# Gather the base from the output itself, ask for the expert weights before the third store, places ahead of gates, scatters in two halves

## The chip, the cores and the metric

One core of one Trainium2 chip runs the whole kernel. The metric is the device time of an execution in microseconds (us). TensorE does the matmuls and transposes, VectorE (DVE), ScalarE (ACT) and GpSimd (POOL) the rest; SyncE (SP) issues most DMAs, GpSimd the indirect ones. Each engine runs its own instruction list in order, and the lists are tied together by semaphores written out by hand.

## The reference, cut to what matters

x is (16, 128, 256): 16 blocks b of 128 channels and 256 positions. Read as rows it is 2048 tokens of 256 values.

```python
# part 1: long convolution of outer products, gated into x
kv  = einsum('bhil,bhjl->bijhl', k, v)            # k = v = ctx, heads of 8
y   = irfft(rfft(kv, 512) * rfft(kernel, 512))[..., :L] + kv * D
x   = x + tanh(g_xattn) * einsum('bijhl,bhil->bjhl', y, layernorm(x))
# part 2: mixture of 8 experts, one per token, capacity 256, and a shared expert
xt = layernorm(x).reshape(2048, 256)
probs = softmax(xt @ Wg); eidx = argmax(probs); gate = probs[eidx]
pos  = (cumsum(onehot) * onehot).sum(-1) - 1; keep = pos < 256
xd   = rows of xt placed at slot eidx * 256 + pos (kept tokens)
oe   = (silu(xd @ W1[e]) * (xd @ W3[e])) @ W2[e]
shared = (silu(xt @ sw1) * (xt @ sw3)) @ sw2
x = x + tanh(g_ffn) * (oe of the token's slot * gate * keep + shared)
```

## The kernel before

The 16 blocks are taken in 4 groups (NG) of 4. The program is a list of slots: slots s = 0 to 31 (CONV) each hold one unit of the convolution (convolve on TensorE, products on VectorE, the kv products of the next group on GpSimd and ScalarE); slots 32 to 50 hold the rest of the shared expert. Inside the slots every step of a group has a due slot (STEPS, for the last group LAST_STEPS): turn the summed terms back and add them to x (turn_r, residual), second layer norm into xrow (ln2), transpose (turn_xT, tokens_low), logits and choice of the expert (choose), gate (gate), place in the expert (places, slot_of_token), scatter.

The steps of the change:

- **Terms and folds.** For groups 2 and 3 the eight terms are folded to four by GpSimd (fold, line 606), one fold a slot; TensorE's turn_r for these groups waits for 8 and for 16 folds.
- **Choice.** gate writes the gate value beside each token's row in xrow (column 256), slot_of_token computes the row numbers dest; its second operation (line 899) frees the PSUM bank of the places, which a later transpose needs. Column 257 of xrow is the token's number (iota). For each of the 4 blocks GpSimd then issues one indirect DMA that scatters 128 rows of 258 floats to xd_scratch (line 639), after it has waited for dest_done and gate_done. For groups 0 to 3 this is due in slots 20, 28, 36 and 42.
- **Shared expert.** Token blocks n = 0 to 7 of 256 tokens: up projection chunks ("gu", n, c), then ("y", n, 0), which VectorE adds to x_sb (line 920). SyncE then stores the two blocks of x_sb twice: to out and to base_scratch (line 549).
- **Experts.** Blocks 8 to 15 are experts 0 to 7. Each weight set is loaded by four DMAs (line 495 twice, 506, 508) into one of 5 buffers that lie in the memory of the terms, so the first load waits for the last turn_r. In SyncE's list the first five experts' loads stand after the stores of n = 2. The weights are split into a high part (ScalarE, weights_high, line 765) and a low part (VectorE, weights_low, line 956) for w = e + 1; w = 1 has its own slot, w = 2 and later follow the first chunk of the expert before. Each matmul of line 1148 runs three times (high x high, low x high, high x low).
- **Rows.** SyncE loads an expert's 256 rows from xd_scratch (load_rows, line 420), the first two after the stores of n = 5 and once all scatters have landed. TensorE transposes them (turn_xe, line 1183; for experts 0 and 1 in slots 49 and 50, from XE_SLOT on), ScalarE and VectorE split them (xe_high, expert_tokens_low), VectorE takes the token numbers from them (tokens_of_slots, tok).
- **Ends.** gather(e) fetches the tokens' rows from base_scratch (line 654), gather(0) waits for all 16 stores; VectorE adds gate times expert output (line 932), and an indirect DMA scatters the sum to out (line 665).

Of the kernel before, what the change touches and what calls it, by code (L numbers as in the profile page):

```python
# [195 lines left out]

def build(nc, x, ctxt, kpad, skip_d, g_x, g_f, wg, w1, w3, w2, sw1, sw3, sw2, out):
    xd = nc.dram_tensor("xd_scratch", (E * CAP, ROW), F32, kind="Internal").ap()
    base = nc.dram_tensor("base_scratch", (B * CH, L), F32, kind="Internal").ap()
    kskip = nc.dram_tensor("kskip_scratch", (H, KPAD), F32, kind="Internal").ap()  # L200
    out_rows = out.rearrange("b c l -> (b c) l")

    with ExitStack() as ctx:
# [265 lines left out]
        def _(sp):  # L469
# [74 lines left out]
                sp.dma_start(xd_flat[k], zeros).then_inc(xd_zeroed, 16)  # L544
            load_ctx(3)
            for n in range(8):
                sp.wait_ge(f_free, FU_AT[("y", n, 0)] + 1)
                for dst in (out, base.rearrange("(b c) l -> b c l", c=CH)):
                    sp.dma_start(dst[2 * n:2 * n + 2].rearrange("b c l -> c b l"),
                                 x_sb[:, 2 * n:2 * n + 2, :]).then_inc(base_stored, 16)  # L550
                if n == 2:
                    for e in range(SETS):
                        load_expert(e)
                if n == 5:
                    for e in range(2):
                        load_rows(sp, e)
# [8 lines left out]
        def _(pool):  # L565
# [35 lines left out]
            def fold(s):  # L601
# [3 lines left out]
                             for i in range(2))  # L605
                pool.tensor_tensor(low, low, high, ALU.add).then_inc(folded, 1)  # L606

            def split_up():
                pool.wait_ge(w_high, 1)
                up = slice(2 * HP, 4 * HP)  # L610
                pool.tensor_tensor(wl_gu[0][:, up], shared_gu[:, up], plain(wh_gu[0][:, up]),
                                   ALU.subtract).then_inc(w_low_pool, 1)

            for s in range(SLOTS):
# [9 lines left out]
                if s == SLOTS - 1:  # L624
                    pool.wait_ge(z_ready, CONV)
                    pool.memset(bg[:, :, :, :], 0.0).then_inc(pool_consts, 1)
                g = due("scatter", s)
                if g >= 0:
                    if g == 0:
                        pool.wait_ge(xd_zeroed, 16 * 4)  # L630
                    if g >= 2:
                        pool.wait_ge(scattered[g % 2], 16 * GB)
                    pool.iota(xrow[:, g % 2, :, L + 1:L + 2], pattern=[[P, GB], [1, 1]], base=1 + g * GB * P,
                              channel_multiplier=1, allow_small_or_imprecise_dtypes=True).then_inc(numbered, 1)
                    pool.wait_ge(numbered, g + 1)
                    pool.wait_ge(dest_done, g + 1)
                    pool.wait_ge(gate_done, g + 1)
                    for b in range(GB * g, GB * (g + 1)):
                        pool.indirect_dma_start(  # L639
                            out=xd, out_offset=bass.IndirectOffsetOnAxis(ap=dest[:, b:b + 1], axis=0),  # L640
                            in_=xrow[:, g % 2, b % GB, :], in_offset=None, bounds_check=E * CAP - 1,
                            oob_is_err=False).then_inc(scattered[g % 2], 16)
                if s == SPLIT_SLOT:
                    split_up()

            def gather(e):
                pool.wait_ge(tok_done, e + 1)
                if e == 0:
                    pool.wait_ge(base_stored, 16 * 16)
                    pool.wait_ge(pool_consts, 6)  # L650
                if e >= BRING:
                    pool.wait_ge(f_free, FU_AT[("y", 8 + e - BRING, 0)] + 1)
                for t in range(2):
                    pool.indirect_dma_start(  # L654
                        out=bg[:, e % BRING, t, :], out_offset=None, in_=base,
                        in_offset=bass.IndirectOffsetOnAxis(ap=tok[:, e, t:t + 1], axis=0),
                        bounds_check=B * CH - 1, oob_is_err=False).then_inc(gathered[e % BRING], 16)

# [12 lines left out]
        def _(act):  # L671
# [104 lines left out]
            for s in range(SLOTS):  # L776
# [20 lines left out]
                    weights_high(1)  # L797
                if s >= XE_SLOT:
                    xe_high(s - XE_SLOT)
            for n in range(SHARED_USES, len(FU)):  # L800
                kind, blk, c = FU[n]
                silu(n)
                if kind == "gu" and c == 0 and blk + 1 < 16:
                    weights_high(blk + 1 - 7)
                if kind == "gu" and c == 1 and 10 <= blk + 1 < 16:
                    xe_high(blk + 1 - 8)

        @block.vector
        def _(dve):
# [186 lines left out]
            for s in range(SLOTS):  # L996
# [18 lines left out]
                    norm_stats(NORM_AT[("ln2", due("ln2_stats", s))])  # L1015
                if due("logits", s) >= 0:
                    choose(due("logits", s))
                if due("gate", s) >= 0:
                    gate(due("gate", s))
                if due("places", s) >= 0:  # L1020
                    slot_of_token(due("places", s))
                if s == SPLIT_SLOT:
                    weights_low(0)
                if s == EXPERT_SPLIT_SLOT:
# [1 line left out]
                if s >= XE_SLOT:  # L1026
                    expert_tokens_low(s - XE_SLOT)
                    tokens_of_slots(s - XE_SLOT)
            for n in range(SHARED_USES, len(FU)):
                kind, blk, c = FU[n]  # L1030
                feed_forward(n)
                if kind == "gu" and c == 0 and blk + 1 < 16:
                    weights_low(blk + 1 - 7)
                if kind == "gu" and c == 1 and 10 <= blk + 1 < 16:
                    expert_tokens_low(blk + 1 - 8)
# [205 lines left out]
```

## Time and profile before

| | |
|---|---|
| median of 3 runs | 228.96 us (228.89 to 229.14) |
| the profiled execution's own time | 228.0 us |
| its span, first to last instruction | 226.2 us |
| mean granted TensorE clock | 0.995 |
| busy: TensorE matmul / VectorE / ScalarE / GpSimd | 88% / 66% / 36% / 56% of the span |
| read / written in HBM | 21.32 / 10.54 MB |

The busy shares are of the whole span. Where the time is set is read from the chain of work that ended last and from what each engine waited for, stage by stage.

### The profile page before, as it was taken

To read this page: it belongs to the slowest core of one execution; us is meant where nothing else is said; L and a number is where in the kernel's file an instruction comes from. 1 tells how busy PE (TensorE), PEld (TensorE's weight loads), DVE (VectorE), ACT (ScalarE), POOL (GpSimd) and SP (SyncE) were. 2 spreads that over 40 slices of the span, in tenths; PEclk is the share of its full clock that TensorE was granted. 3 is DMA by queue.
4 is the path that set the end of the run, shared out by engine and by line. 5 is a ranking of instruction groups with operands and counts; after the bars stand their busy time and mean duration, and the time that the engine had idled before them with its cause. 6 is when DMAs were issued, how large, how long until landed. Compare 5 with 4: busy or idle time off the path is not lost.

```text
span 226.2 us, 3954 instructions
## 1 busy us (share of the span) xinstructions
PE 198.4 (88%) x1344; PEld 178.9 (79%) x1344; DVE 150.3 (66%) x483; ACT 80.7 (36%) x153; POOL 126.6 (56%) x129
## 2 busy tenths in 40 slices
PE   0399999969999898999989969997989999999970
PEld 0267789748998797898989959995989999999960
DVE  5868986699789885589855663752547755676240
ACT  2425314163460844033320653620352444234200
POOL 3797863395847489413690216083055677776651
PEclk9999999999999999999999999999999999999997
DMA  4799993000000010021300199995454888522221
GB/s 123 257 234 351 360 412 142 0 0 4 3 3 0 23 71 3 0 94 51 114 23 3 49 326 362 347 359 169 137 163 131 260 280 257 180 71 82 66 79 46
DMA packets 24101, 31.87 MB, mean 141 GB/s; under 512 B 3390, under 2 KB 21574, under 8 KB 24080
## 3 DMA queue, kind: packets, MB, share of 16 engines
q1 hardware_dynamic: 21424, 24.75, 33.7%
q0 software_dynamic: 2304, 6.05, 8.1%
q10 hardware_dynamic: 352, 0.81, 1.1%
q8 instruction: 11, 0.18, 0.3%
q14 instruction: 10, 0.08, 0.1%
HBM read 21.32 MB, written 10.54 MB: 141 GB/s over the span
## 4 chain that ended last, share of the span: by engine, by line
PE 66%; DVE 12%; DMA 8%; issue 5%; ACT 3%; POOL 2%; POOLq 1%; ACTq 0%; DVEq 0%; SPq 0%
PE fb L1148 13%; PE z L1148 10%; PE tp L1087 10%; PE z L1062 10%; PE z L1172 8%; PE z L1059 6%; DVE terms L452 5%; PE fb L1172 5%; DMA kskip_scratch<-kp 3%; DMA toep<-kskip_scratch 2%; DVE wl_gu L956 2%; DVE stats L824 2%; PE tp L1183 2%; POOL xd_scratch L639 1%; DMA xd_scratch<-xrow,dest 1%
## 5 line engine op out<-in xcount | busy, mean ns | idle before, releaser
L452 DVE TENSOR_TENSOR terms<-z,qr 128x512 f32<-128x512 f32 (+2 forms) x192 | 49.1, 326 | 8.0 <-PE z L1062 7.9
L1062 PE MATMUL z<-kv,toep 128*128 128x288 f32 x128 | 42.5, 415 | 0.0
L433 POOL TENSOR_TENSOR kv<-ct 128x768 f32<-128x768 f32 x15 | 28.2, 1883 | 13.9 <-PE z L1062 10.8
L1148 PE MATMUL fb<-xTh,wh_gu 128*128 128x256 f32 (+1 forms) x104 | 32.4, 312 | 0.7 <-issue 0.7
L1059 PEld LDWEIGHTS z<-kv,toep 128*128 128x128 f32 x128 | 22.7, 196 | 11.5 <-issue 7.7
L654 POOL DMA_INDIRECT kv<-base_scratch,tok x16 | 22.4, 1397 | 15.8 <-DMA base_scratch<-x_sb 11.3
L639 POOL DMA_INDIRECT xd_scratch<-xrow,dest x16 | 17.0, 1064 | 25.0 <-DVE dest L905 21.3
L1059 PE MATMUL z<-kv,toep 128*128 128x144 f32 x128 | 28.0, 302 | 2.9 <-DVE terms L452 2.4
L1148 PE MATMUL fb<-xTl,wh_gu 128*128 128x256 f32 (+1 forms) x104 | 29.1, 279 | 0.0
L1148 PE MATMUL fb<-xTh,wl_gu 128*128 128x256 f32 (+1 forms) x104 | 29.0, 279 | 0.0
L606 POOL TENSOR_TENSOR terms<-terms 128x512 f32<-128x512 f32 x16 | 20.2, 1282 | 11.3 <-DVE terms L452 11.3
L1148 PE MATMUL z<-xTh,wh_gu 128*128 128x256 f32 (+1 forms) x88 | 25.6, 291 | 0.8 <-DVE wl_gu L956 0.8
L1087 PE MATMUL tp<-ident,terms 128*128 128x128 f32 x192 | 23.0, 277 | 1.9 <-DVE terms L452 1.0
L1148 PE MATMUL z<-xTl,wh_gu 128*128 128x256 f32 (+1 forms) x88 | 24.5, 278 | 0.0
L1148 PE MATMUL z<-xTh,wl_gu 128*128 128x256 f32 (+1 forms) x88 | 24.4, 278 | 0.0
L1087 PEld LDWEIGHTS tp<-ident,terms 128*128 128x128 f32 x192 | 22.2, 193 | 2.5 <-DVE terms L452 1.2
L665 POOL DMA_INDIRECT out<-kv,tok x16 | 16.1, 1004 | 12.8 <-DVE kv L932 8.3
L744 ACT ACTIVATE sg<-fb 128x256 f32<-128x256 f32 (+1 forms) x26 | 9.8, 376 | 31.6 <-PE fb L1148 31.6
L1062 PEld LDWEIGHTS z<-kv,toep 128*128 128x128 f32 x128 | 20.6, 195 | 0.0
L1148 PEld LDWEIGHTS fb<-xTh,wh_gu 128*128 128x128 f32 (+1 forms) x104 | 19.3, 186 | 1.6 <-issue 0.9
L1148 PEld LDWEIGHTS fb<-xTh,wl_gu 128*128 128x128 f32 (+1 forms) x104 | 19.3, 185 | 0.8
L1148 PEld LDWEIGHTS fb<-xTl,wh_gu 128*128 128x128 f32 (+1 forms) x104 | 19.3, 186 | 0.0
(121 smaller groups left out, 377.9 us busy)
## 6 DMA issues: line engine op xcount, KB each, us to landing
terms<-w SPq DMA_DIRECT2D x16, 352.0 KB, 4.7
ct<-ctxt SPq DMA_DIRECT2D x3, 768.0 KB, 7.3
xd_scratch<-xrow SPq DMA_DIRECT2D x4, 516.0 KB, 9.4
kv<-xd_scratch SPq DMA_DIRECT2D x8, 258.0 KB, 3.5
out<-x_sb SPq DMA_DIRECT2D x8, 256.0 KB, 2.3
base_scratch<-x_sb SPq DMA_DIRECT2D x8, 256.0 KB, 2.9
terms<-w SPq DMA_DIRECT2D x8, 256.0 KB, 4.9
x_sb<-x SPq DMA_DIRECT2D x3, 512.0 KB, 6.1
```

The costliest lines, as they stand in the source:

```text
L433: eng.tensor_tensor(dst, left, right, ALU.mult)
L452: return eng.tensor_tensor(view(terms, t0 + row * TROW + col, [[64, 2], *td]), view(src, zo, [[512, 2], *zd]), view(qr, q0 + qo, [[CW, 2], ...
L606: pool.tensor_tensor(low, low, high, ALU.add).then_inc(folded, 1)
L639: pool.indirect_dma_start(out=xd, out_offset=bass.IndirectOffsetOnAxis(ap=dest[:, b:b + 1], axis=0), in_=xrow[:, g % 2, b % GB, :], in_off ...
L654: pool.indirect_dma_start(out=bg[:, e % BRING, t, :], out_offset=None, in_=base, in_offset=bass.IndirectOffsetOnAxis(ap=tok[:, e, t:t + 1] ...
L665: pool.indirect_dma_start(out=out_rows, out_offset=bass.IndirectOffsetOnAxis(ap=tok[:, e, t:t + 1], axis=0), in_=fin[:, e % 2, t, :], in_o ...
L744: act.activation(sg[0:n, k % SGS, :], bank[0:n, 0:256], ACT.Silu).then_inc(silu_done, 1)
L1059: pe.matmul(view(z[s % 2], k * 512 + GB, [[PL, NPL], [1, GB]]), toep[:, h, P:2 * P], view(kv, o, [[PL, NPL], [1, GB]]), start=True, stop=F ...
L1062: mm = pe.matmul(z[s % 2][:, k, 0:KVH], toep[:, h, 0:P], view(kv, o, [[1, KVH]]), start=False, stop=True, skip_group_check=True)
L1087: mm = pe.matmul(tp[n % 2][:, j * P:(j + 1) * P], src, ident[:, :], is_transpose=True, start=(t == 0), stop=(t == terms_of(g) - 1))
L1148: mm = pe.matmul(bank[0:rows(blk, c), m * 256:(m + 1) * 256], wt[w % 2][:, col:col + rows(blk, c)], xt[:, place, k, first:first + 256], st ...
L1172: mm = pe.matmul(bank[:, t * L:(t + 1) * L], hidden(blk, c)[0:rows(blk, c), t * P:(t + 1) * P], down[0:rows(blk, c), c * L:(c + 1) * L], s ...
```

## The change

Four edits.

1. base_scratch and its eight stores are gone; the gathers read the rows from out, and gather(0) waits for eight stores.
2. In SyncE's list the loads of the first five experts stand before the wait for ("y", 2, 0) and its store, not after it.
3. VectorE computes the places of a group before its gates. The split of expert 1's weights (w = 2) goes into the slots: its high part on ScalarE after xe_high(0), in slot XE_SLOT = 49, its low part on VectorE at the end of the last slot, 50, after tokens_of_slots(1).
4. The scatters of groups 0 to 2 go out in two halves: blocks 0 and 1 in the due slot, blocks 2 and 3 in the next one, behind that slot's kv products and fold. The last group's four stay together.

```diff
-    base = nc.dram_tensor("base_scratch", (B * CH, L), F32, kind="Internal").ap()
...
             for n in range(8):
-                sp.wait_ge(f_free, FU_AT[("y", n, 0)] + 1)
-                for dst in (out, base.rearrange("(b c) l -> b c l", c=CH)):
-                    sp.dma_start(dst[2 * n:2 * n + 2].rearrange("b c l -> c b l"),
-                                 x_sb[:, 2 * n:2 * n + 2, :]).then_inc(base_stored, 16)
                 if n == 2:
                     for e in range(SETS):
                         load_expert(e)
+                sp.wait_ge(f_free, FU_AT[("y", n, 0)] + 1)
+                sp.dma_start(out[2 * n:2 * n + 2].rearrange("b c l -> c b l"),
+                             x_sb[:, 2 * n:2 * n + 2, :]).then_inc(base_stored, 16)
...
+            def scatter(g, parts):
+                for b in parts:
+                    n = GB * g + b
+                    pool.indirect_dma_start(
+                        out=xd, out_offset=bass.IndirectOffsetOnAxis(ap=dest[:, n:n + 1], axis=0),
+                        in_=xrow[:, g % 2, b, :], in_offset=None, bounds_check=E * CAP - 1,
+                        oob_is_err=False).then_inc(scattered[g % 2], 16)
...
                 g = due("scatter", s)
+                if 0 <= due("scatter", s - 1) < NG - 1:
+                    scatter(due("scatter", s - 1), range(2, GB))
...
-                    for b in range(GB * g, GB * (g + 1)):
-                        pool.indirect_dma_start(
-                            out=xd, out_offset=bass.IndirectOffsetOnAxis(ap=dest[:, b:b + 1], axis=0),
-                            in_=xrow[:, g % 2, b % GB, :], in_offset=None, bounds_check=E * CAP - 1,
-                            oob_is_err=False).then_inc(scattered[g % 2], 16)
+                    scatter(g, range(GB if g == NG - 1 else 2))
...
-                    pool.wait_ge(base_stored, 16 * 16)
+                    pool.wait_ge(base_stored, 16 * 8)
...
-                        out=bg[:, e % BRING, t, :], out_offset=None, in_=base,
+                        out=bg[:, e % BRING, t, :], out_offset=None, in_=out_rows,
...
                 if s >= XE_SLOT:
                     xe_high(s - XE_SLOT)
+                if s == XE_SLOT:
+                    weights_high(2)
...
-                if kind == "gu" and c == 0 and blk + 1 < 16:
+                if kind == "gu" and c == 0 and 10 <= blk + 1 < 16:
                     weights_high(blk + 1 - 7)
...
+                if due("places", s) >= 0:
+                    slot_of_token(due("places", s))
                 if due("gate", s) >= 0:
                     gate(due("gate", s))
-                if due("places", s) >= 0:
-                    slot_of_token(due("places", s))
...
                     tokens_of_slots(s - XE_SLOT)
+                if s == SLOTS - 1:
+                    weights_low(2)
...
-                if kind == "gu" and c == 0 and blk + 1 < 16:
+                if kind == "gu" and c == 0 and 10 <= blk + 1 < 16:
                     weights_low(blk + 1 - 7)
```

## Rows read from the trace of the kernel before

**Rows 1.** The page's chain of work that ended last, by engine.

```profile
PE 66%; DVE 12%; DMA 8%; issue 5%; ACT 3%; POOL 2%; POOLq 1%; ACTq 0%; DVEq 0%; SPq 0%
```

**Rows 2.** The chain in order of time, from 112 us: start, us, what.

```profile
117.48 0.87 issue
...
152.03 3.07 DMA xd_scratch<-xrow,dest
...
155.16 2.66 DMA kv<-xd_scratch
```

**Rows 3.** TensorE's timeline where it waited: start, us, what [idle before <- releaser].

```profile
75.29 0.66 PE L1074 MATMUL tp<-ident,xn 128*128 128x128 f32 x4 [0.76 <-DVE t L899]
...
89.42 2.02 PE L1087 MATMUL tp<-ident,terms 128*128 128x128 f32 x16 [1.01 <-DVE terms L452]
...
133.30 0.66 PE L1097 MATMUL tp<-ident,xrow 128*128 128x128 f32 x4 [1.71 <-DVE t L899]
...
157.95 0.63 PE L1183 MATMUL tp<-ident,kv 128*128 128x128 f32 x4 [1.67 <-DMA kv<-xd_scratch]
...
166.49 0.36 PE L1148 MATMUL z<-xTh,wh_gu 128*128 128x256 f32 x1 [0.78 <-DVE wl_gu L956]
```

**Rows 4.** GpSimd's timeline, 85 to 119 us.

```profile
85.58 6.19 POOL L606 TENSOR_TENSOR terms<-terms 128x512 f32<-128x512 f32 x5
...
108.29 1.07 POOL L639 DMA_INDIRECT xd_scratch<-xrow,dest  x1 [3.21 <-DVE dest L905]
...
112.23 0.97 POOL L639 DMA_INDIRECT xd_scratch<-xrow,dest  x1 [0.30 <-issue]
113.22 5.03 POOL L606 TENSOR_TENSOR terms<-terms 128x512 f32<-128x512 f32 x4
```

**Rows 5.** Timelines of VectorE and GpSimd, 131 to 154 us.

```profile
131.93 0.42 DVE L915 TENSOR_TENSOR hT<-z,sg 128x256 f32<-128x256 f32 x1 [3.66 <-ACT sg L744]
...
134.69 1.28 DVE L943 TENSOR_TENSOR xTl<-tp,xTh 128x512 fp32r<-128x512 f32 x2
...
146.14 0.17 DVE L905 CAST dest<-slotf 128x4 int32<-128x4 f32 x1
...
147.99 1.61 DVE L956 TENSOR_TENSOR wl_gu<-terms,wh_gu 128x1408 fp32r<-128x1408 f32 x1
...
147.14 0.99 POOL L639 DMA_INDIRECT xd_scratch<-xrow,dest  x1 [7.11 <-DVE dest L905]
148.44 2.01 POOL L639 DMA_INDIRECT xd_scratch<-xrow,dest  x1 [0.30 <-issue]
```

**Rows 6.** Busy time by stretch; the last two columns are DMA share and GB/s.

```profile
118.00:122.00 4.00, 3.65 (x33) 3.69 (x34) 1.18 (x2) 0.15 (x1) 0.24 (x1) 1.00 0.01 4
...
150.00:154.00 4.00, 4.00 (x36) 3.95 (x35) 1.24 (x3) 1.04 (x3) 3.39 (x4) 1.00 0.91 318
```

**Rows 7.** Timelines of ScalarE and VectorE, 158 to 167 us.

```profile
158.62 0.60 ACT L750 ACTIVATE xTh<-tp 128x512 fp32r<-128x512 f32 x1 [4.50 <-PE tp L1183]
...
163.32 1.37 ACT L765 ACTIVATE wh_gu<-terms 128x1408 fp32r<-128x1408 f32 x1
...
163.08 0.16 DVE L964 SCALAR_TENSOR_TENSOR tok<-tv,kv 128x2 int32<-128x2 f32 x1
...
164.72 1.63 DVE L956 TENSOR_TENSOR wl_gu<-terms,wh_gu 128x1408 fp32r<-128x1408 f32 x1 [0.79 <-ACT wh_gu L765]
```

**Rows 8.** The page's DMA issues: operation, count, KB each, median us to landing.

```profile
out<-x_sb SPq DMA_DIRECT2D x8, 256.0 KB, 2.3
base_scratch<-x_sb SPq DMA_DIRECT2D x8, 256.0 KB, 2.9
```

**Rows 9.** SyncE's timeline, the first and the last of the 20 weight issues.

```profile
129.24 1.03 SPq L495 DMA_DIRECT2D terms<-w  x2
...
140.39 1.25 SPq L508 DMA_DIRECT2D terms<-w  x1
```

**Rows 10.** Line 639's landing times: the four scatters of group 1, then of group 3.

```profile
DMA to landing us min/median/max: 2.6/2.7/2.9
...
DMA to landing us min/median/max: 3.1/4.3/4.9
```

## The prediction

> **What bounds the kernel now.** I read the page's chain first [rows 1]: TensorE holds 66% of it, so most of the span is matmul time that this change doesn't touch. I then listed the chain in order of time from 112 us and looked only for pieces that aren't TensorE [rows 2]. Three places matter to this diff.
>
> First, TensorE waits twice for GpSimd. Before the residual transposes of group 2 it is idle 1.01 us [rows 3], and before those of group 3 the chain has 0.87 us at 117.48 [rows 2]. Both times GpSimd works without a pause from its first scatter (77.07 and 108.29) to the fold that is awaited: the third of the five from 85.58, at 85.58 + 3 x 6.19/5 = 89.3, and the last of the four from 113.22, at 118.25 [rows 4].
>
> Second, the stretch from the last group's places to the first expert. Group 3's dest is ready at 146.3, the four scatters run from 147.14 to 153.0, the last lands 3.07 us after its start, then SyncE asks for expert 0's rows (2.66 us to landing), and TensorE transposes them at 157.95 after 1.67 us of nothing [rows 2, 3, 5]. In that stretch the reader should see two handicaps: the second scatter takes 2.01 us where the others take 0.97, and it stands inside VectorE's 1.61 us weight split of line 956 [rows 5]; and the DMA engines are still 0.91 busy from 150 to 154, though idle from 118 to 122 [rows 6].
>
> Third, at 166.49 TensorE has waited 0.78 us for the low part of expert 1's weights (line 956) [rows 3]. After that the chain is TensorE without a gap, to expert 7's last matmul at 219.1.
>
> **The change, part by part.** The sum goes against the profiled execution: 228.0 us, span 226.2. The median of the three runs shown is 228.96, so I carry the difference 0.96 over to the forecast.
>
> *Expert 1's split earlier.* ScalarE made the high part at 163.32, behind the first expert silu, and VectorE the low part at 164.72, to about 166.35 [rows 7]. Now the high part stands behind xe_high(0), which ends at 159.2; its inputs are there (expert 1's loads are issued by 134, and the shared up-projection of block 7, the last reader of that half, ran before 153.7). It takes 1.37 us, to 160.6, and fits ahead of xe_high(1) at 161.65. The low part stands behind tok of expert 1, that is from 163.24, takes 1.63 and ends at 164.87. TensorE finishes the last chunk of expert 0 at 166.49 - 0.78 = 165.71, so its wait is gone: **-0.78**. Queued behind the low part is hT of (8,0), 163.51 before and 164.85 now; its readers are y of expert 0 (TensorE, 169.9) and the silu ring, both after 167. Covered by more than 2 us.
>
> A rule of the Trainium skill ("SBUF — State Buffer", section "SBUF: two separate sides") speaks against this move: VectorE with two SBUF inputs and GpSimd share a port pair that is locked for a whole instruction, whoever starts first, and the other blocks fully. The second scatter agrees, 2.01 against 0.97 us. By the rule a gather that started ahead of the split could push it back by up to 1 us and take back some 0.3 of the 0.78; but the gather can't start before y(7)'s store, issued at 162.07, has landed (2.3 us in the median [rows 8]), about 164.4, so the split is first.
>
> *No base copy.* Eight stores of 256 KB and their issues (0.47 to 0.53 us each on SyncE) go. The gathers wait for 8 stores, not 16; gather(0) started at 166.10, behind the last base store, and starts some 1.3 us earlier. Nothing waits: its reader at 172.7 has the data at about 171.6. Worth 0 by itself. The rows read are those of out before any expert scatter of the same token, so no new wait appears.
>
> *Weights ahead of the third store.* load_expert(0) waits for the last residual transposes, done at 122.2; before, it stood behind y(2)'s store at 128.30 and was issued at 129.24. Twenty issues take from 129.24 to 141.64, 12.4 us [rows 9], so now 122.2 to 134.6. Behind them in SyncE's queue stands y(2)'s store (ready at 128.3, issued about 134.6) and y(3)'s (134.8); only the gathers, 30 us later, wait for these. The first reader of the weights, at 145.97, never waited, so the earlier loads are worth nothing directly. Their worth is that with seven us of head start and 1.5 MB of base copies less the DMA engines are free when group 3 is scattered: 5.3 MB of weights and three 0.26 MB stores at about 350 KB/us end near 140. Scatters on idle engines land in 2.6 to 2.9 us (group 1), in the busy stretch in 3.1 to 4.9 [rows 10]. Only the last one is on the chain: 3.07 becomes about 2.7, **-0.4** (bounds 0 and -0.5). The load of expert 0's rows had 2.66, already the least of its kind, 0. The 1.04 us of the second scatter stay: the split of line 956 comes after the silu at 147.2 and meets it again.
>
> For that last scatter the Trainium skill ("DMA: Bandwidth & Descriptors", section "Anatomy of one DMA — SWDGE (gpsimd) path") gives 2.0 us plus bytes over 436 KB per us: for 132 KB 2.3 us, which would make this term -0.8. The rows of idle engines show 2.6 at the least, so the row is used.
>
> *Places ahead of gates.* Three gate operations and six places operations stand one behind the other on VectorE and end at 146.3 [rows 5]; the gates are 0.56 us of them. GpSimd waits for both results, and their sum is the same in either order: 0 for the scatters. What comes earlier by 0.56 us is the release of the transpose bank (line 899), for which TensorE waited 0.76 at 75.29 and 1.71 at 133.30 [rows 3]. Neither pays. At 75 what comes next is GpSimd's stretch from 77.07, which sets TensorE's start at 89.42 and begins when dest and gate are both done. At 133, TensorE's next need is the low part of the tokens, which VectorE ends at 135.97 after working from 131.93 without a pause [rows 5]; a permutation inside that stretch doesn't move its end. TensorE waits there longer instead. **0**; bounds -0.6 and 0.
>
> *Scatters in halves.* For groups 0 to 2 two scatters go out, then the next slot's products and fold, then two more. For group 2 nothing stands between. For 0 and 1 the same work has to be done before the awaited fold (scatters four, folds up to number 23 and up to 31), only in another order, so the end moves only by what a switch costs. Inside a run of scatters each one follows 0.30 us after the other's end; from scatter to fold there is no gap (112.23 + 0.97 = 113.20, fold at 113.22) [rows 4]. The trace has no scatter right behind a fold. Bounds: the 0.30 vanishes under the fold (-0.3 a group), or a restart costs what one costs after a wait, 0.83 from dest at 146.31 to 147.14 [rows 5], that is +0.5 a group. I take **0**, the 0.30 staying where it is: it stands ahead of a scatter after another scatter, and the nearest case is the same instruction.
>
> Sum: -0.78 - 0.4 = -1.2; 228.0 becomes 226.8, and with the 0.96 the median becomes **227.8 us**, -0.5%. Within 0.2% (0.46 us) a measurement of this kernel hardly tells from no change.
>
> **Rivals.**
> (a) *The halves pay.* If the switch hides the 0.30 twice, and the earlier bank release brings anything, both waits for GpSimd shrink: 227.8 - 0.6 = 227.2, at most 226.6. For it: both stretches really end in a wait of TensorE (1.01 and 0.87). Against: nothing shows the gap hidden.
> (b) *Only one term comes.* The last scatter still lands in 3.1 because y(5)'s store at 150.42 is beside it (228.2); or TensorE's 0.78 returns as another wait a slot later, say on hidden tiles that the split pushed back (228.6). For it: VectorE is at 2.7 of 4 us there. Against: more than 2 us of cover.
> (c) *The change does nothing that can be measured*: the expert stretch is TensorE-bound, and the 1.67 us wait is of fixed latencies; 228.6 to 229.2.
> (d) *Slower: the switch from fold to scatter.* If the sequencer prepares a scatter only after the fold before it has ended, each of the two stretches grows by 0.5, plus some 0.2 because the first scatter of a run is longer (1.07 against 0.97 [rows 4], 1.19 in group 0); TensorE waits for both: 227.8 + 1.4 = 229.2. Slower than before it is from 0.6 us a switch, by over 0.2% from 0.8. The order of cost is there, the size isn't.
>
> **How the numbers follow.** Forecast (227.4 to 228.2) 0.55; (a) 0.14; (b) 0.17, of which a quarter is within 0.2%; (c) 0.07; (d) 0.07. Faster by over 0.2%: 0.55 + 0.14 + 0.13 = 0.82, from which I take 0.02 for a term that I don't see, 0.80; same, 0.04 of (b) and 0.07 of (c) and what (d) leaves under 0.2%, 0.14; slower 0.06. The range runs from (a)'s worth with part of the bank release, 226.9, to the second case of (b), 228.7; beyond stand the rest of (c) and (d).
>
> **What the profile after should show.** Twenty weight issues from 122.2; DMA share low by 142 to 150; the last scatter landing in 2.6 to 2.8; TensorE's wait before line 1183 at 1.2 to 1.3 us, not 1.67; the split for expert 1 starting near 163 and no wait of TensorE on line 956; VectorE's row for line 899 ahead of 884, and longer waits of TensorE where the bank release comes early; the folds awaited at 89.3 and 118.3 at the same times within 0.3. The prediction is wrong if a scatter after a fold starts over 0.6 us after it, if hT of (8,0) shows up as a releaser of TensorE, or if y(5)'s store still stretches the last scatter.

## The result, and the profile after

The changed kernel takes 226.22 us in the median of four executions (225.65 to 227.72), the kernel before 229.05 beside it; the ratio is 0.9898, 95% interval 0.9862 to 0.9934. Two repeats gave 0.9921 (0.9897 to 0.9945) and 0.9942 (0.9920 to 0.9964). So it is faster, by 0.6 to 1.0%; forecast were 0.5% and 227.8 us, and the measured 226.22 lies under the range. In 16 of 112 executions of the kernel before TensorE's mean granted clock is 0.981 to 0.984 (0.989 to 0.996 in the others) and the time about 2.4 us longer; the ratios leave only seven of these out, but without them its medians would move by 0.2 us at most.

The profiled executions seem at first to contradict this: span 226.2 us before, 226.0 after. They have to be cut at common points. The chain of the changed kernel, around its start and around the first expert (start, us, what):

```profile
4.51 7.71 DMA kskip_scratch<-kp
...
12.66 5.86 DMA toep<-kskip_scratch
...
153.50 2.48 DMA xd_scratch<-xrow,dest
...
156.04 2.70 DMA kv<-xd_scratch
...
158.88 0.63 PE tp L1191 x4
```

Before, the same start had these two lines:

```profile
4.46 6.15 DMA kskip_scratch<-kp
...
10.63 4.27 DMA toep<-kskip_scratch
```

The 24 KB store of kskip took 1.6 us longer after, and the Toeplitz load behind it 1.6 us longer too; nothing of the change stands there. Five marks, the starts of these instructions in each trace, divide an execution: group 0's first residual transpose ("start"), group 3's first residual transpose, the first scatter of group 3, expert 0's transposes, expert 2's transposes, the last output sum of VectorE.

| stretch, us | before | after | after, repeats (2) |
|---|---|---|---|
| start | 31.66 | 33.34 | 32.32, 32.73 |
| to group 3's residual | 86.69 | 86.63 | 86.60, 86.63 |
| to its first scatter | 28.79 | 28.68 | 28.88, 28.81 |
| to expert 0's transposes | 10.81 | 10.23 | 10.35, 10.42 |
| to expert 2's transposes | 11.37 | 10.31 | 10.32, 10.32 |
| to the last sum | 49.86 | 49.81 | 49.81, 49.85 |
| behind the start, together | 187.52 | 185.66 | 185.96, 186.03 |

A further trace of the kernel before has 187.23 behind its start of 32.90. So the change is worth 1.5 us behind the start (means 187.4 and 185.9), and nearly all of it lies in two stretches. The start itself has no part in the change: over seven traces of the kernel before and its variants it averages 32.3 us, over eight of the changed kernel and its variants 32.3 as well (e8, e9 and e11, which edit the start, left out). What is left of the recorded 2.8 us I come to at the end.

Where TensorE waited, after (its timeline; the rows answer to those of [rows 3]):

```profile
76.39 0.66 PE L1082 MATMUL tp<-ident,xn 128*128 128x128 f32 x4 [0.19 <-DVE t L905]
80.38 1.06 PE L1105 MATMUL tp<-ident,xrow 128*128 128x128 f32 x8 [0.46 <-ACT qr L711]
91.08 2.02 PE L1095 MATMUL tp<-ident,terms 128*128 128x128 f32 x16 [1.01 <-DVE terms L451]
...
134.35 0.66 PE L1105 MATMUL tp<-ident,xrow 128*128 128x128 f32 x4 [1.15 <-DVE t L905]
137.69 0.36 PE L1156 MATMUL fb<-xTh,wh_gu 128*128 128x256 f32 x1 [1.29 <-issue]
...
158.88 0.63 PE L1191 MATMUL tp<-ident,kv 128*128 128x128 f32 x4 [1.12 <-DMA kv<-xd_scratch]
```

The bank release pays nothing: the wait for it falls by 0.57 and 0.56 us, and the next wait takes it (0.46 ahead of the transposes at 80.38; 1.29 ahead of the matmul at 137.69, before 0.70). The wait for the fold is 1.01 as before. The wait for expert 0's rows falls from 1.67 to 1.12. The wait on the low part of expert 1's weights is gone; no row of TensorE stands there.

GpSimd's timeline after, with the halves of group 1 (answers to [rows 4]):

```profile
87.25 6.20 POOL L604 TENSOR_TENSOR terms<-terms 128x512 f32<-128x512 f32 x5
...
109.99 1.07 POOL L609 DMA_INDIRECT xd_scratch<-xrow,dest  x1 [3.24 <-DVE xrow L896]
111.36 0.98 POOL L609 DMA_INDIRECT xd_scratch<-xrow,dest  x1 [0.30 <-issue]
112.34 1.30 POOL L604 TENSOR_TENSOR terms<-terms 128x512 f32<-128x512 f32 x1
113.81 0.99 POOL L609 DMA_INDIRECT xd_scratch<-xrow,dest  x1 [0.17 <-issue]
115.11 0.97 POOL L609 DMA_INDIRECT xd_scratch<-xrow,dest  x1 [0.30 <-issue]
116.10 3.77 POOL L604 TENSOR_TENSOR terms<-terms 128x512 f32<-128x512 f32 x3
```

A scatter behind a fold follows it by 0.17 us. From the first scatter to the end of the last awaited fold it was 9.96 us (108.29 to 118.25) and is 9.88 (109.99 to 119.87). TensorE's wait of 1.01 us at 91.08 names VectorE, but VectorE's terms end at 90.25, and the third of the five folds from 87.25 ends at about 91.0 (87.25 + 3 x 6.20/5): it waits for the fold, as before.

VectorE's timeline at the moved split (answers to [rows 7]):

```profile
164.00 0.16 DVE L970 SCALAR_TENSOR_TENSOR tok<-tv,kv 128x2 int32<-128x2 f32 x1
164.20 1.63 DVE L962 TENSOR_TENSOR wl_gu<-terms,wh_gu 128x1408 fp32r<-128x1408 f32 x1
165.74 0.75 DVE L921 TENSOR_TENSOR hT<-fb,sg 128x256 f32<-128x256 f32 x2
```

The low part starts right behind tok and ends at 165.83, and no one waits for the hidden tiles (hT) behind it. The first gather starts at 166.08, behind the split, as forecast. The DMA engines (busy by stretch, last two columns share and GB/s; answers to [rows 6]):

```profile
126.00:130.00 4.00, 4.00 (x28) 3.74 (x26) 3.49 (x19) 1.80 (x4) 1.35 (x3) 1.00 1.01 346
...
146.00:150.00 4.00, 4.00 (x30) 3.82 (x30) 2.75 (x13) 1.93 (x3) 1.05 (x2) 1.00 0.19 66
150.00:154.00 4.00, 4.00 (x33) 3.87 (x33) 2.25 (x3) 0.55 (x2) 3.39 (x3) 1.00 0.43 146
```

0.91 has become 0.43 from 150 to 154, while the last scatters are out, and the last one lands in 2.48 us, not 3.07.

### The profile page after: what moved, and what is told of

It is laid out like the page before. It is cut to its first block, busy times and chain, and to the rows that moved or that the text cites. A ratio compares the mean times of both kernels' runs of the same rounds, so it can differ in the third digit from the quotient of the medians.

```text
span 226.0 us, 3947 instructions
## 1 busy us (share of the span) xinstructions
PE 196.6 (87%) x1344; PEld 178.0 (79%) x1344; DVE 150.1 (66%) x483; ACT 80.9 (36%) x153; POOL 126.1 (56%) x129
## 4 chain that ended last, share of the span: by engine, by line
PE 63%; DMA 10%; DVE 10%; issue 6%; ACT 5%; POOL 3%; POOLq 1%; ACTq 0%; SPq 0%; DVEq 0%
PE fb L1156 13%; PE tp L1095 10%; PE z L1156 10%; PE z L1070 9%; PE z L1180 8%; PE z L1067 5%; PE fb L1180 5%; DVE terms L451 4%; DMA kskip_scratch<-kp 3%; DMA toep<-kskip_scratch 3%; ACT xrow L681 2%; DVE stats L830 2%; PE tp L1191 2%; POOL xd_scratch L609 1%; POOL rstd L576 1%
## 5 line engine op out<-in xcount | busy, mean ns | idle before, releaser
L1070 PE MATMUL z<-kv,toep 128*128 128x288 f32 x128 | 42.0, 410 | 0.0
L1067 PEld LDWEIGHTS z<-kv,toep 128*128 128x128 f32 x128 | 22.4, 193 | 12.3 <-issue 8.4
L1067 PE MATMUL z<-kv,toep 128*128 128x144 f32 x128 | 27.3, 296 | 4.5 <-DVE terms L451 2.4
L658 POOL DMA_INDIRECT kv<-out,tok x16 | 22.2, 1387 | 14.4 <-DMA out<-x_sb 9.8
L1070 PEld LDWEIGHTS z<-kv,toep 128*128 128x128 f32 x128 | 20.3, 192 | 0.0
```

The source lines that it names most:

```text
L658: pool.indirect_dma_start(out=bg[:, e % BRING, t, :], out_offset=None, in_=out_rows, in_offset=bass.IndirectOffsetOnAxis(ap=tok[:, e, t:t ...
L1067: pe.matmul(view(z[s % 2], k * 512 + GB, [[PL, NPL], [1, GB]]), toep[:, h, P:2 * P], view(kv, o, [[PL, NPL], [1, GB]]), start=True, stop=F ...
L1070: mm = pe.matmul(z[s % 2][:, k, 0:KVH], toep[:, h, 0:P], view(kv, o, [[1, KVH]]), start=False, stop=True, skip_group_check=True)
```

## The experiments

All times are medians. The experiments ran in four sets, each beside its own executions of the kernel before, whose medians were 228.74 (e1 to e4), 228.50 (e5 to e8), 228.39 (e9 to e12) and 228.20 (e13 to e16). Times are best compared within a set. "Behind the start" is the sum of the table above.

**e1, e12: the changed kernel again.**

> The changed kernel once more, beside the kernel before in the same rounds, to split the 2.8 us of the result. In the two profiled executions the stretch from 60 us to the end is shorter by 1.9 us, and the start is longer by 1.7. Theory A (the four edits give the 1.9; the start of the kernel, where a 24 KB store and the first Toeplitz load hold the chain, varies from execution to execution by chance): the time is 1.5 to 2.3 us below before, and the single times of both kernels scatter by 1 us or more. Theory B (leaving out the base tensor also makes the start faster, by another memory layout): again 2.6 to 3.0 below, with the kernel before always the slower in the start.

> The changed kernel a third time, as the measure for the three others of this call and for the size of the change itself: by the stretches of the traces 1.6 to 1.9 us below before, with the start varying by 1 us and more from execution to execution in both.

226.78 and 227.13 us, ratios as above. The start was 32.32 and 32.73, later than in the first trace of before. Theory A holds for the size in e1 (2.0 below before); in e12 the medians are 1.3 apart and the traces 1.2 to 1.5 behind the start, a little under the 1.6 to 1.9 expected. The single times scatter by 1 us and more in e12 (226.01 to 227.57) and at first (225.65 to 227.72), by 0.6 in e1.

**e2, e4: the base copies or the head start?** e2 is the kernel before with the first edit:

```diff
-                for dst in (out, base.rearrange("(b c) l -> b c l", c=CH)):
-                    sp.dma_start(dst[2 * n:2 * n + 2]...
+                sp.dma_start(out[2 * n:2 * n + 2]...
...
-                        out=bg[:, e % BRING, t, :], out_offset=None, in_=base,
+                        out=bg[:, e % BRING, t, :], out_offset=None, in_=out_rows,
```

> The kernel before with the first edit alone: no base tensor, no base stores, gathers from the output. Theory A: the last scatter of group 3 still lands amid weight loads, a little sooner; 0 to 0.4 us below before. Theory B: 0.9 to 1.4 us below before, and the kskip store lands in 6 us or less after its issue.

e4 is the kernel before with the loads of the first five experts ahead of the third store:

```diff
+                if n == 2:
+                    for e in range(SETS):
+                        load_expert(e)
                 sp.wait_ge(f_free, FU_AT[("y", n, 0)] + 1)
...
-                if n == 2:
-                    for e in range(SETS):
-                        load_expert(e)
```

> The kernel before with the expert loads ahead of the third store, alone; base copies stay. Theory A: the DMA engines are free by 150 us but for y(5)'s two stores, the last scatter lands in 2.5 to 2.7 us, 0.4 to 0.6 below before. Rival D (it is the base copies, not the head start, that stretched the last scatter): less than 0.2 below before.

e2: 228.04, ratio 0.9965 (0.9942 to 0.9989); the last scatter lands in 2.36. e4: 228.36, ratio 0.9978 (0.9951 to 1.0005); it lands in 2.68. The chain's rows for that scatter, e2 and then e4:

```profile
152.39 2.36 DMA xd_scratch<-xrow,dest
```

```profile
153.75 2.68 DMA xd_scratch<-xrow,dest
```

Either edit frees it; they don't add. The stretch from first scatter to transposes was 10.69 and 10.72, against 10.81 and 10.68 in the two traces of the kernel before: no gain that can be told. The second scatter took 2.33 and 2.29 us there, not 2.01, and in e2 expert 0's rows 2.93, not 2.66. With before's second scatter they would be 10.37 and 10.44, as in the changed kernel. Neither theory B's 0.9 us nor its store of 6 us or less (6.49) came.

**e3: the split of expert 1 alone.**

```diff
                     xe_high(s - XE_SLOT)
+                if s == XE_SLOT:
+                    weights_high(2)
...
-                if kind == "gu" and c == 0 and blk + 1 < 16:
+                if kind == "gu" and c == 0 and 10 <= blk + 1 < 16:
                     weights_high(blk + 1 - 7)
...
                     tokens_of_slots(s - XE_SLOT)
+                if s == SLOTS - 1:
+                    weights_low(2)
...
```

> The kernel before with expert 1's weight split moved ahead, alone. From the aligned traces the pair from TensorE's transposes at 157.95 to 169.49 shrinks by 1.06 us, not by the 0.78 that TensorE's idle row showed. Theory A and B: 1.06 below before (1.0 to 1.1 in the trace). Rival C (the row is right): 0.78.

The stretch from expert 0's to expert 2's transposes is 10.34 against 11.37: 1.03 us, as theory A and B said, not rival C's 0.78. The time is 227.24, ratio 0.9925 (0.9897 to 0.9953), 1.5 below before and so more than 1.03, but that trace's own sum behind the start fell by only 0.56, as the scatters' stretch came out at 11.29. For one edit's size the stretch is the measure, not the median.

**e5: places ahead of gates and halves alone.**

```diff
+                if 0 <= due("scatter", s - 1) < NG - 1:
+                    scatter(due("scatter", s - 1), range(2, GB))
...
+                    scatter(g, range(GB if g == NG - 1 else 2))
...
+                if due("places", s) >= 0:
+                    slot_of_token(due("places", s))
                 if due("gate", s) >= 0:
                     gate(due("gate", s))
```

> The kernel before with places ahead of gates and scatters in halves, alone. My account: the scatter behind a fold follows it by 0.17 us, not 0.30, so each of the two awaited folds ends 0.1 us earlier at most; from the first residual transposes of group 0 to those of group 3 86.6 us against 86.7, and in time within 0.3 us of before. Rival (the earlier bank release pays where TensorE waited 0.76 and 1.71 us): 0.6 to 1.2 us below before.

229.10, ratio 1.0025 (0.9988 to 1.0061). 86.65 to group 3's residual and 28.70 to its scatter, 0.13 us less in sum than the first trace of the kernel before and 0.03 less than the second. Five of the 12 executions have the lower clock (0.982 to 0.985); the others' median is 228.1, beside 228.3 for the kernel before taken in the same way. The rival, that the bank release pays 0.6 us or more, is out.

**e6: the base tensor back in the changed kernel.**

```diff
+    base = nc.dram_tensor("base_scratch", (B * CH, L), F32, kind="Internal").ap()
...
+            sp.dma_start(base[0:1, :], x_sb[0:1, 15, :]).then_inc(base_stored, 16)
...
-                    pool.wait_ge(base_stored, 16 * 8)
+                    pool.wait_ge(base_stored, 16 * 9)
```

> The changed kernel with the base tensor declared again and one row of 1 KB stored to it at the end of the stores (the first gather waits for it too). Theory A (the tensor has no part in the start of the kernel): the same as the changed kernel, 1.6 to 2.1 us below before. Theory B (leaving the tensor out made the start faster): 0.8 to 1.2 us below before.

226.51, ratio 0.9872 (0.9813 to 0.9931), behind the start 185.68. 2.0 below before in its set, the same as the changed kernel; the tensor has no part in it. Theory B falls.

**e7, e10, e14: expert 0's split away from the second scatter.** One constant, in the changed kernel (e7), in the changed kernel with the loads back behind the third store (e10), and in the kernel before (e14):

```diff
-EXPERT_SPLIT_SLOT = CONV + 12
+EXPERT_SPLIT_SLOT = CONV + 7
```

> The changed kernel with expert 0's weight split five slots earlier (its slot CONV + 7 in place of CONV + 12), so that the second scatter of group 3 has no split of VectorE beside it. If that overlap is what makes the scatter take 2.0 to 2.3 us: it takes 0.98, the stretch from the first scatter of group 3 to expert 0's transposes shrinks from 10.3 to 9.3 us, and the time is 0.9 to 1.1 below the changed kernel. Rival (the second scatter of a run is long for another reason, or VectorE's work ahead of the logits makes the scatters start later by as much): less than 0.3 below it.

> The kernel with expert 0's split in slot CONV + 7 and the expert loads back behind the third store. If the early loads are worth most as what allows an early split: ScalarE waits for expert 0's weights in slot 38 at about 136 to 138, TensorE's next groups stand behind it, and half or more of the 1.2 us is lost again. Rival (the weights are there in time anyway): as fast as with early loads, but for 0.2 to 0.5 us at the last scatter.

> The kernel before with expert 0's split in slot CONV + 7 alone, loads still late and base copies kept. TensorE's wait ahead of expert 0's transposes falls from 1.7 to 1.9 us to 0.6 to 0.8, for no other reason than the second scatter. Theory E (the long wait is what drops the clock in some executions): no execution 2 us above the rest, median 1.0 below before. Rival F (the clock drops by chance of the chip): the high ones are there as often as before.

e7: 225.62, ratio 0.9848 (0.9788 to 0.9908). GpSimd's timeline in e7, the last scatter of group 2 and the first two of group 3:

```profile
139.81 2.28 POOL L609 DMA_INDIRECT xd_scratch<-xrow,dest  x1 [0.30 <-issue]
...
147.93 0.99 POOL L609 DMA_INDIRECT xd_scratch<-xrow,dest  x1 [5.65 <-DVE xrow L896]
149.23 0.97 POOL L609 DMA_INDIRECT xd_scratch<-xrow,dest  x1 [0.30 <-issue]
```

and VectorE's:

```profile
139.63 1.62 DVE L962 TENSOR_TENSOR wl_gu<-terms,wh_gu 128x1408 fp32r<-128x1408 f32 x1
```

The long scatter went along with the split: it is now group 2's last, which nobody waits for, and group 3's second takes 0.97. The stretch is 9.03, against 10.05 to 10.42 in the five traces with the four edits and the split in its old slot (after, e1, e6, e8, e12); the time is 0.9 below e6 of the same set.

The traces say what holds the scatter up. In all 18 the one long scatter starts inside VectorE's split, and it ends 0.84 to 0.86 us after the split's end, however early it started: it takes 1.97 us where it starts 0.5 behind the split's start, and 2.33 where it starts 0.13 behind. So its length is set by where it meets the split, which is why it reads 1.97 to 2.33 from kernel to kernel. The gathers of the experts do the same (2.1 to 2.5 us, ending 0.87 to 0.93 behind a split). The other way round nothing is held up. Here a gather starts just ahead of a split (after, GpSimd's row and then VectorE's), runs beside it to its end, and the split takes 1.65 us where 1.61 to 1.63 are usual:

```profile
184.05 1.04 POOL L658 DMA_INDIRECT kv<-out,tok  x1 [0.30 <-issue]
```

```profile
184.07 1.65 DVE L962 TENSOR_TENSOR wl_gu<-terms,wh_gu 128x1408 fp32r<-128x1408 f32 x1 [0.84 <-ACT wh_gu L769]
```

The rule of the Trainium skill that the prediction weighed ("SBUF — State Buffer", section "SBUF: two separate sides") is a port pair that VectorE, in an instruction with two SBUF inputs, and GpSimd share, locked for a whole instruction by whichever starts first. The page limits it to a GpSimd instruction that reads SBUF, a condition that the prediction left out. The long scatters and gathers agree with it. The other half, that the first to start blocks the other, whoever it is, does not show: the measured split isn't blocked by a gather that started first. So the 0.3 us that the prediction feared from such a gather had no ground here, whatever the order.

e10: 225.61, ratio 0.9889 (0.9863 to 0.9914), the stretch 9.29. ScalarE did not wait for expert 0's weights (its split ran at 135.19, the load was issued at 128.82), so my first reading falls and the rival holds: once the base copies are gone the early loads are worth 0.3 us at most here (9.29 against 9.03 in e7; e9, with early loads, has 9.35).

e14: 228.00, ratio 0.9980 (0.9951 to 1.0008): next to nothing, where I expected 1.0. The second scatter did shrink to 0.97, but the last one then started earlier, among the loads and copies, and landed in 4.2 us (chain):

```profile
151.19 4.21 DMA xd_scratch<-xrow,dest
```

with the DMA engines 1.08 busy from 146 to 150, where e10 has 0.84. TensorE's wait was 1.83 and not 0.6 to 0.8. The stretch was 10.98, no shorter than before's. So one long scatter hid another cost: with the loads late and the copies kept, the busy DMA engines take back what the shorter scatter gave.

**e8, e11, e9: the start.** Group 1's x is loaded behind the kskip store, in the changed kernel (e8), the kernel before (e11), and with e7's edit (e9):

```diff
-            load_x(1)
             sp.wait_ge(skip_added, 1)
             sp.dma_start(kskip, kp[:, :]).then_inc(skip_stored, 16)
+            load_x(1)
             sp.wait_ge(skip_stored, 16)
```

> The changed kernel with the load of group 1's x issued after the 24 KB kskip store, not ahead of it. If the landing of that store (6.2 to 7.8 us from issue in six executions) is set by transfers queued ahead of it, and is what scatters in the start: the store lands in 3 to 5 us, the first residual transposes come 1 to 2 us earlier, near 31, and the time is 1 to 2 us below the changed kernel. Rival (the store waits for the context load of the other queue, or the Toeplitz load behind it takes the time back): within 0.5.

> The kernel before with only the load of group 1's x behind the kskip store. If the start has nothing to do with the change, the same gain as on the changed kernel: the store lands in about 5 us, the first residual transposes near 31 us, the time 1 to 1.5 us below before.

> The changed kernel with both later edits together: expert 0's split in slot CONV + 7 and group 1's x loaded behind the kskip store. Each works in its own stretch (143 to 157 us and the first 32 us), so they should add: 1.2 us from the first and 1.3 from the second, 223.6 to 224.3 us, the fastest of all. Rival (the start's gain is only luck of its six executions): no faster than the first of the two alone, 225.6.

e8: 225.13, ratio 0.9815 (0.9756 to 0.9873), the store lands in 5.03, the start is 31.05. e11: 227.18, ratio 0.9967 (0.9939 to 0.9996), start 31.39. e9: 225.08, ratio 0.9854 (0.9829 to 0.9879), start 31.54 and 184.82 behind it. The medians are 1.4 below the changed kernel of the same set (e8 against e6) and 1.2 below before (e11), so the edit is worth something in the start, on either kernel; how much is open. The store landed in about 5 us only in e8; it took 5.8 in e11 and 5.9 in e9, and e16 has 5.9 without the edit. And e9 did not reach the 223.6 to 224.3 that the sum gave: it is level with e8, and 0.5 us below e7, not 1.3, a step between sets that the ratios to before (0.9854 and 0.9848) don't show at all. The start of e9's chain is not the store but the context load, which the moved x doesn't help:

```profile
1.79 6.56 DMA ct<-ctxt
```

The kernel before as it is can have that too: in e13's trace its chain also begins with the context load (6.94 us). e9 is 3.3 us below before in its set.

**e13, e15, e16: does a long wait drop the clock?** e11's trace was odd: behind the start 189.62, most of the excess over the 187.2 and 187.5 of the kernel before between expert 0's and expert 2's transposes (13.05, not 11.37). TensorE's rows there, and the granted clock (third column from the right):

```profile
158.11 0.73 PE L1183 MATMUL tp<-ident,kv 128*128 128x128 f32 x4 [1.94 <-DMA kv<-xd_scratch]
158.63 1.91 PE L1172 MATMUL z<-shared_down,hT 128*128 128x256 f32 x4
```

```profile
154.00:158.00 4.00, 2.17 (x11) 1.56 (x9) 1.18 (x2) 0.00 (x0) 0.71 (x1) 1.00 0.43 126
158.00:162.00 4.00, 3.89 (x13) 3.24 (x14) 0.93 (x3) 0.60 (x1) 0.00 (x0) 0.57 0.42 142
162.00:164.00 2.00, 2.00 (x16) 1.85 (x14) 0.75 (x1) 0.52 (x1) 0.00 (x0) 1.00 0.00 0
```

After 1.94 us without a matmul TensorE runs at the lower of its two levels, 1.2 GHz, for part of four microseconds; four matmuls that take 1.03 us elsewhere take 1.91, and the drop costs 13.05 - 11.37 = 1.7 us. e15 and e16 lengthen this wait in the changed kernel by putting half or all of GpSimd's clearing of bg ahead of the last scatter (e16's edit; e15 leaves the other half where it was):

```diff
-                if s == SLOTS - 1:
-                    pool.wait_ge(z_ready, CONV)
-                    pool.memset(bg[:, :, :, :], 0.0).then_inc(pool_consts, 1)
...
-                    scatter(g, range(GB if g == NG - 1 else 2))
+                    scatter(g, range(GB - 1 if g == NG - 1 else 2))
+                    if g == NG - 1:
+                        pool.wait_ge(z_ready, CONV)
+                        pool.memset(bg[:, :, :, :], 0.0).then_inc(pool_consts, 1)
+                        scatter(g, [GB - 1])
```

> The kernel before against itself: ratio 1. Some of its single times should lie some 2 us above the rest, as in earlier rounds (a fifth above 229.9), and the rest near 228.4. If its profiled execution is one of the high ones, TensorE's granted clock is down for a few us right after expert 0's transposes and nowhere else.

> The changed kernel with half of GpSimd's clearing of the gather buffers (0.9 us) between the third and the last scatter of group 3, so that TensorE waits some 1.9 to 2.0 us ahead of expert 0's transposes, as the kernel before did at its longest. Theory E: the high executions come back, some 1.7 us on top, in a share of the executions; the others 0.9 above the changed kernel. Rival F: all 0.9 above it.

> The same with all of the clearing (1.84 us) between the two scatters: a wait of 2.7 to 2.9 us. Theory E: the clock drops in all or nearly all executions, 1.84 + 1.7 = 3.5 us above the changed kernel, near 230.2. Rival F: 1.84 above it, near 228.6, with few or no high ones.

e13: 227.99, ratio 0.9990 (0.9958 to 1.0021); one of 12 executions is high (230.34, mean clock 0.982). Its trace is a normal one, with a wait of 1.54. e15: 227.90, ratio 0.9968 (0.9939 to 0.9996), a wait of 1.88; its highest is 228.62, but that one and the 228.41 have a mean clock of 0.986, where its others have 0.989 and more. e16: 229.42, a wait of 2.77; 8 of 12 executions lie at 229.3 to 230.9, 4 at 227.7 to 228.4. The eight have mean clocks of 0.983 to 0.987, the four 0.991 to 0.993, and the medians of the two lots are 1.7 us apart. Its trace has the drop, and 12.01 us between the two transposes where the changed kernel has 10.3:

```profile
158.72 0.63 PE L1192 MATMUL tp<-ident,kv 128*128 128x128 f32 x4 [2.77 <-DMA kv<-xd_scratch]
```

```profile
158.00:162.00 4.00, 3.28 (x12) 2.80 (x13) 0.93 (x3) 1.86 (x2) 0.00 (x0) 0.71 0.39 132
162.00:166.00 4.00, 4.00 (x28) 3.61 (x28) 1.95 (x5) 0.98 (x2) 0.00 (x0) 0.86 0.14 47
```

So a longer wait brings the drop (e16 against all others), in most executions but not in all, which is why the median stayed under theory E's 230.2. Rival F would have put e16 near 228.6 with few high ones.

The kernel before as it is was never traced in such an execution, but the record has the mean clock of every execution of the four sets, and it sorts them. Waits are those ahead of expert 0's transposes in each kernel's one trace (two for the kernel before):

| kernels | wait in the trace, us | executions with a mean clock of 0.987 or less |
|---|---|---|
| before (four sets and e13) | 1.67, 1.54 | 16 of 112 |
| e3, e5, e11, e14, e15 | 1.84, 1.60, 1.94, 1.83, 1.88 | 2 of 13, 5 of 12, 3 of 12, 0 of 12, 2 of 12 |
| e16 | 2.77 | 8 of 12 |
| after, e1, e12, e2, e4, e6 to e10 | 0 to 1.31 | 0 of 72 |

No kernel with a short wait had one. It isn't the wait of 1.71 us at 133.30 [rows 3] that does it: e2 and e4 keep that wait (1.71) and have none, e5 has it at 1.21 and has five. A wait of the old length brings the drop in some executions and isn't enough by itself (e14 has none). In the kernel before such executions are 2.4 us longer in the mean; 1.7 is what the drop costs in the two traces that have it, the rest isn't shown.

## Why the prediction was right in its mechanism and wrong in its number

- **Expert 1's split** (forecast -0.78): right in kind, mis-sized by 0.25 us or more. Between the transposes of experts 0 and 2 it brought 1.03 to 1.06 us (after, e1, e12, e3). The row's 0.78 counts from the modelled end of the last matmul. Matmuls are pipelined: they stand 0.11 us apart though each is given 0.28. The two around the wait start at 165.44 and 166.49, 1.05 apart where 0.11 is usual, that is 0.94 lost, and the one after the wait is followed at 0.20 rather than at 0.11. Together that is 1.03, the measured sum.
- **Weights early and no base copy** (forecast -0.4): right. The twenty weight issues begin at 123.81, or 122.1 with the later start taken off, against 122.2 forecast. The last scatter lands in 2.36 to 2.48 (forecast 2.7); the mean stretch shrank by 0.4, part of the landing's gain going to the second scatter, which took 1.98, 2.18 and 2.23 in the three traces of the changed kernel. What I had not seen is that either edit alone frees the landing (e2, e4), and that they matter more in company of an earlier split (e14 against e10 and e7). The fit of the Trainium skill ("DMA: Bandwidth & Descriptors", section "Anatomy of one DMA — SWDGE (gpsimd) path") gives, as an estimate, 2.3 us for this scatter. The rows show 2.36 in seven of the ten traces without the copies whose chain has it, and 2.45 to 2.48 in the others, closer to it than to the 2.6 that I took as the least.
- **Places ahead of gates** (0): right, for the reasons given; e5 and both waits above show it.
- **Halves** (0, bounds -0.6 and +1.0): 0 to -0.1. The gap behind a fold is 0.17, between no gap and the 0.83 of a restart, my two bounds. Rival (a) and rival (d) are both out.
- **Rivals (b) and (c)**: out; both terms came, none was taken back.

These terms give 1.5 us, 0.3 more than forecast, and would put the time at 227.5: inside the range. The recorded 226.22 is 1.3 lower still, and the step that failed there is the first one of the sum, "I carry the difference 0.96 over to the forecast". It treats the median of before and the start of the kernel as fixed. They aren't, and the recorded pair drew before high and the changed kernel low: before's medians in five sets of executions were 229.05, 228.74, 228.50, 228.39 and 228.20, the changed kernel's 226.22, 226.78 and 227.13. The start alone, to the first residual transpose, took from 31.44 to 33.34 us in the 15 traces of kernels whose start is the same list of instructions as before's, and the kskip store in it landed in 5.9 to 7.8 us. In ten of the 15 the chain runs over that store; in others it begins elsewhere, as with the first Toeplitz load (7.8 us in e1 and e7) or the context load (6.94 in e13). A range of 226.9 to 228.7 made of the change's terms alone left that out.

How the recorded 2.8 us divide is thus settled in part: 1.5 us are in the stretches, and in repeats the medians are 1.3 and 2.0 apart. The other 1.3 us are no work of the change that any trace shows. They don't come from the low clock: the four executions of before took 228.89 to 229.49, and the shortest with a low clock in the sets behind took 229.96. What is left is the variation of single executions, of which the start is the part that the traces show; that four executions of each kernel fell 2.8 us apart and not 1.5 was luck. How much each part gave there can't be told; they have one trace a kernel. A gain that the forecast had no term for at all is that the changed kernel no longer has low-clock executions, which is worth some 0.3 us in before's mean but at most 0.2 in its median.

## What to carry to other kernels

Cut two traces at common instructions before comparing spans: here both spans were 226 us, and 1.5 us of gain stood behind 1.7 us of a slower start. Price a TensorE wait by the distance between starts, not by the idle figure, which counts from modelled ends. When two things slow one chain (a scatter held up by VectorE's split, and a busy set of DMA engines), mending one may only move the next step into the other: on the kernel before the early split alone gave 0.2 us, less than the measurement tells, on the changed kernel 0.9.

## What the runs showed of the hardware that I had not expected

- A scatter on GpSimd that starts inside a two-input split of VectorE ends 0.84 to 0.86 us after the split does: 1.97 to 2.33 us instead of 0.97, a cost of 1.0 to 1.4, which follows the split wherever it is moved (e7, e9, e10, e14). A split that starts inside a gather isn't held up (1.65 us).
- After 1.94 and 2.77 us without a matmul TensorE's granted clock fell to its lower level for some three to four microseconds and cost 1.7 us; after 1.54 to 1.88 us, in the traces here, it did not, but by the mean clocks it did in some untraced executions of the kernels with such waits, and in none of 72 of the kernels with shorter ones.
- A 24 KB store at the start, with half a megabyte of loads issued ahead of it, lands in 5.9 to 7.8 us in 15 traces (6.2 and 7.4 in the two of the kernel before).
